# Transformer block with adaptive layer norm: exponentials' sums grouped up to the diagonal on GpSimd, splits of q and k moved to ScalarE and VectorE

## What is computed

```python
mod = silu(condition) @ Wada + bada                      # shift, scale, gate, twice
sh_a, sc_a, gt_a, sh_m, sc_m, gt_m = jnp.split(mod, 6, axis=1)
xm = layernorm(x) * (1.0 + sc_a[:, None, :]) + sh_a[:, None, :]
q, k, v = split heads of (xm @ Wqkv)                     # 16 heads of 32
scores = where(causal, q @ k.T * hd ** -0.5, -inf)
x = x + gt_a * ((softmax(scores) @ v) @ Wproj + bproj)
xm = layernorm(x) * (1.0 + sc_m[:, None, :]) + sh_m[:, None, :]
x = x + gt_m * (gelu(xm @ W1 + b1) @ W2 + b2)
```

## Time and profile before

| | |
|---|---|
| three executions | 3172.76, 3175.78 (median), 3176.37 us |
| span of the profiled execution | 3170.2 us |
| TensorE matmul busy | 3123.6 us, 99% |
| VectorE, GpSimd, ScalarE busy | 74%, 55%, 38% |
| one attention body with a block (13 of them) | 92.1 us |
| of that, GpSimd busy in 700 to 792 us | 76.6 us |

### The profile page before, as it was taken

One profiled execution on the slowest core, in us unless ns is written; L12 is line 12 of the kernel. 1 busy time (PEld: TensorE's weight loads), 2 busy tenths in 40 slices (PEclk: granted clock), 3 DMA queues, 4 the chain that ended last, 5 costly groups with the idle time before them and its releaser, 6 DMA issues.

```text
span 3170.2 us, 68318 instructions
## 1 busy us (share of the span) xinstructions
PE 3123.6 (99%) x24936; PEld 2518.4 (79%) x24936; DVE 2343.5 (74%) x2981; ACT 1196.1 (38%) x2354; POOL 1747.6 (55%) x1385
## 2 busy tenths in 40 slices
PE   7999999999999999999999999999999999999999
PEld 5677777777777777766688888989888898988888
DVE  4688887887888787766876777777677777767673
ACT  3355555555555555566521221212112121211111
POOL 3288888888888888888843333333332333323232
PEclk9999999999999999999999999999999999999999
DMA  6766666666656665666612312122221313122120
GB/s 241 217 185 192 173 191 185 180 181 186 195 171 191 186 182 168 195 194 171 167 57 64 75 44 79 40 79 56 63 75 44 79 40 79 56 63 74 45 66 14
DMA packets 304627, 391.85 MB, mean 124 GB/s; under 512 B 24296, under 2 KB 206088, under 8 KB 304448
## 3 DMA queue, kind: packets, MB, share of 16 engines
q1 hardware_dynamic: 292336, 371.86, 41.3%
q10 hardware_dynamic: 12112, 17.42, 1.6%
HBM read 270.66 MB, written 118.00 MB: 123 GB/s over the span
## 4 chain that ended last, share of the span: by engine, by line
PE 89%; DVE 5%; issue 2%; POOL 1%; ACT 1%; DMA 1%; SPq 0%; ACTq 0%; DVEq 0%; POOLq 0%
PE psH L1014 22%; PE psY L1024 22%; PE psA L793 9%; PE psT L847 8%; PE psA L885 7%; PE psP L922 6%; PE psA L797 6%; PE psS L816 4%; DVE mx L1364 2%; PE psA L858 2%; PE psA L765 1%; DVE psS L1360 1%; PE psA L907 1%; PE psA L902 1%; PE psA L847 1%
## 5 line engine op out<-in xcount | busy, mean ns | idle before, releaser
L1637 POOL TENSOR_TENSOR h_l<-h_full,h_h 128x256 fp32r<-128x256 f32 x512 | 488.9, 955 | 1073.5 <-DVE h_h L1537 1073.5
L1364 DVE TENSOR_REDUCE mx<-psS 128x4 f32<-128x2048 f32 (+3 forms) x384 | 665.9, 1755 | 119.5 <-PE psS L816 81.7
L1116 ACT ACTIVATE e<-psT 128x512 f32<-128x512 f32 (+1 forms) x1202 | 605.6, 554 | 375.0 <-PE psT L847 371.8
L1239 ACT ACTIVATE h_full<-psH,b1c 128x256 f32<-128x256 f32 x512 | 243.0, 475 | 1216.8 <-PE psH L1014 1216.8
L1014 PE MATMUL psH<-a_l,w1p_h 128*128 128x256 f32 x2048 | 576.1, 281 | 0.0
L1014 PE MATMUL psH<-a_h,w1p_l 128*128 128x256 f32 x2048 | 575.9, 281 | 0.0
L1014 PE MATMUL psH<-a_h,w1p_h 128*128 128x256 f32 x2048 | 574.1, 280 | 1.0 <-ACT o_sb L1124 0.8
L1695 POOL TENSOR_TENSOR es<-e 128x512 f32<-128x512 f32 (+1 forms) x242 | 446.7, 1847 | 159.3 <-ACT e L1116 75.4
L1537 DVE CAST h_h<-h_full 128x256 fp32r<-128x256 f32 x512 | 179.6, 351 | 399.5 <-ACT h_full L1239 396.8
L847 PEld LDWEIGHTS psT<-qst,kst 97*128 97x128 f32 x2404 | 349.0, 189 | 113.6 <-issue 70.7
L847 PE MATMUL psT<-qst,kst 97*128 97x256 f32 (+1 forms) x2404 | 410.4, 290 | 3.2 <-ACT e L1116 1.7
(11 more groups left out here) (120 smaller groups left out, 5211.2 us busy)
## 6 DMA issues: line engine op xcount, KB each, us to landing
qk_split<-qk_hl SPq DMA_DIRECT2D x128, 512.0 KB, 3.6
kst<-qk_split SPq DMA_DIRECT2D x128, 256.0 KB, 3.9
qst<-qk_split SPq DMA_DIRECT2D x128, 256.0 KB, 4.1
xin<-in_x_dram SPq DMA_DIRECT2D x64, 256.0 KB, 3.5
values<-vout ACTq DMA_DIRECT2D x64, 256.0 KB, 2.4
kmx<-qk_split SPq DMA_DIRECT2D x32, 512.0 KB, 4.7
qmx<-qk_split SPq DMA_DIRECT2D x32, 512.0 KB, 5.9
kst<-qk_split SPq DMA_DIRECT2D x128, 128.0 KB, 3.9
```

Source lines behind the costliest of these rows:

```text
L1116: act.activation(e[:, s % ERING, 2 * hp:2 * hp + 2, 0:w], score_bank(s, hp, with_a)[:, :, 0:w], ACT.Exp, scale=SCALE).then_inc(sem("exp_do ...
L1239: act.activation(h_full[:, m % 4, :], psH[:, m % 4, 0:RA], ACT.Gelu, bias=b1c[:, m:m + 1])\
L1364: reduce = dve.tensor_reduce(mx[:, part, :, qt], psS[:, :, col:col + w], AX_X, ALU.max)
L1637: return pool.tensor_tensor(dst, full, high.bitcast(F32), ALU.subtract)
```

## The change

Three things change, all within the bodies with a block.

1. The groups become (0,1,2,3), (4,5,6), (7,8), (9). The diagonal slots 3, 6 and 8 are now later slots of a group: each gets a `half_add` of 1024 elements before its 512-element addition. So GpSimd does 12 additions of 1024 elements in a half in place of 9. No group ends off the diagonal any more, so `added_sums` falls away in these bodies (3 in a half), and `diagonal_sums` for slots 3, 6 and 8 runs 4 x 256 columns on `es` in place of 2 x 4 x 128 on `e` and `es`.
2. The high part of q and k is taken by ScalarE (`a_high`: a copy, as it already is in the beginning) in the step in which VectorE took it.
3. The low part is subtracted by VectorE (`a_low`), in the step in which GpSimd did, and a store of q and k waits for VectorE's semaphore.

```diff
-SUM_GROUPS = {True: [(0, 1, 2), (3,), (4, 5)] + [(i,) for i in range(6, SLOTS)], False: [(i,) for i in range(SLOTS)]}
+SUM_GROUPS = {True: [(0, 1, 2, 3), (4, 5, 6), (7, 8), (9,)], False: [(i,) for i in range(SLOTS)]}
...
-                sp.wait_ge(sem("a_lo_done"), ia * A_NLO + n + 1)
+                if isinstance(ia, int) and ia < AHEAD:
+                    sp.wait_ge(sem("a_lo_done"), ia * A_NLO + n + 1)
+                else:
+                    sp.wait_ge(sem("a_lo_body"), (ia - AHEAD) * A_NLO + n + 1)
...
+            def a_high(ia, n):
+
+                act.wait_ge(sem("a_copied"), ia * A_ITEMS + n + 1)
+                act.activation(qk_hl[:, n % QK_RING, HIGH[n % 2]].bitcast(F32R), qk_hl[:, n % QK_RING, LOW[n % 2]],
+                               ACT.Copy).then_inc(sem("qk_hi"), 1)
...
+                    item = formed(u, s, 1, HIGH_LATE, with_a, after_a)
+                    if item and item[1] < A_NQK:
+                        a_high(*item)
                     if r in PLACE_AT and not (last and h + PLACE_AT[r][0] == 2):
...
-            def a_high(ia, n):
+            def a_low(ia, n):
 
                 if n < A_NQK:
-                    dve.wait_ge(sem("a_copied"), ia * A_ITEMS + n + 1)
-                    full = qk_hl[:, n % QK_RING, LOW[n % 2]]
-                    dve.tensor_tensor(qk_hl[:, n % QK_RING, HIGH[n % 2]].bitcast(F32R), full, full, ALU.max)\
-                       .then_inc(sem("qk_hi"), 1)
+                    dve.wait_ge(sem("qk_hi"), ia * A_NQK + n + 1)
+                    at = qk_hl[:, n % QK_RING, LOW[n % 2]]
+                    dve.tensor_tensor(at.bitcast(F32R), at, qk_hl[:, n % QK_RING, HIGH[n % 2]],
+                                      ALU.subtract).then_inc(sem("a_lo_body"), 1)
...
-                    item = formed(u, s, 1, HIGH_LATE, with_a, after_a)
+                    item = formed(u, s, 1, LOW_LATE, with_a, after_a)
                     if item:
-                        a_high(*item)
+                        a_low(*item)
...
-                    item = formed(u, s, 1, LOW_LATE, with_a, after_a)
-                    if item:
-                        a_low(*item)
```

More of the change, by code:

```diff
@@ L1194, in wqkv_high @@
                 act.activation(wqkv_h[:, :, cols], wqkv[:, :, cols], ACT.Copy).then_inc(sem("wqkv_hi"), 1)
[L1196 to L1200, removed]
             wqkv_high(0)
@@ L1211, in _ @@
                     if n < A_NQK:
-                        a_high_alone(ia, n)
+                        a_high(ia, n)
                     if n > A_NQK:
```

## The result

The changed kernel takes 3181.37 us (median of 11 runs, 3181.11 to 3184.88), the kernel before 3174.04 in the same rounds. The ratio is 1.0025 with a 95% interval of 1.0016 to 1.0034: 7 us slower. The sign is what I forecast, at a third of the size; the largest part of the loss came from another mechanism.

A forecast was written before the change was run, and what follows sets the result against it. TensorE was taken as the bound, its matmuls filling 99% of the span. Per body -2.76 + 1.35 + 0.35 + 1.85 + 0 + 0.8 + 0.3 = +1.9 us, over 12 bodies +22.8: 3198.5 us, range 3164 to 3220.

The forecast's parts named there:

- The sum: All gains and stalls of a body with a layer norm: +1.9 us, in 12 bodies +22.8 us.
- What TensorE is spared: Six `added_sums` of 0.46 us fall away in each body: 2.76 us off; joined diagonal matmuls gain 0.
- GpSimd's chain, steps 9 and 15: At slots 3 and 6, TensorE waits for GpSimd's masks and additions: stalls of 1.35 and 0.35 us.
- D: How much later TensorE stands than before: +0.9 us after step 9, +0.8 after step 15; also the forecast itself, chance 0.50.
- Step 19: At slot 8, behind `a_rstd`, TensorE stalls 2.15 us for GpSimd's chain, against 0.31 before: 1.85 more.
- the 746.7 for the chain without collisions: In step 19, GpSimd's chain without collisions ends at 746.7 and TensorE waits 1.06 us, 0.75 more than before.
- Step 39: At slot 8, the chain alone gives 0.1 us, two splits of the block about 0.9; taken as 0.8 (0.1 to 1.6).
- Meetings of VectorE and GpSimd: VectorE's instructions with two SBUF inputs do not overlap GpSimd's; each costs a backlogged GpSimd 0.47 us, layer-norm ones 0.2.
- rival B: VectorE becomes a bound as well, TensorE waiting for its maxima: +2.9 us a body, 3211 us; chance 0.15.
- Step 23: ScalarE's copy stands ahead of `a_modulate`, for which TensorE already waits: 0.3 us added (0 to 0.6).
- Rival A: Saved matmuls win because VectorE's instructions mostly find gaps in GpSimd's list: -1.2 us a body, 3160 us; chance 0.22.

The follow-up runs named there:

- the last two experiments: Changed kernel with the modulation ahead of the copy on ScalarE and only slot 6, or slots 3 and 6, joined: 0.9981 and 0.9974 of the kernel before.

## Why the prediction was right or wrong

The sum failed in two of its terms. GpSimd's chain, forecast at 4.35 us of stalls a body (steps 9, 15, 19 and 39), cost 1.31; and the wait of TensorE for VectorE's maxima, put at nothing, cost 1.75. One by one:

- **What TensorE is spared**: right. 6 x 0.46 was 6 x 0.44, and the joined diagonal matmuls cost nothing either way.
- **GpSimd's chain, steps 9 and 15** (1.35 and 0.35 us): wrong, 0 and 0 in the changed kernel. The chain was about as late as I had it: the addition of slot 3 ends 18.0 us behind the body's first addition, where I had 18.6. But TensorE wants it only at 18.7, because VectorE has made it 1.3 us late by then. The chain does cost where that is taken away: 0.44 in step 9 and 0.53 in step 15 with the first subtraction moved, 0.74 and 0.53 with the block's low part as zeros. TensorE stood 0.9 us later than before at the end of step 15, where I had D at 0.8: that is luck, since VectorE had made it late and not GpSimd.
- **Step 19** (2.15 us of stall): mis-sized, about 0.9. From the end of `a_rstd` at 745.13 to L910 at 750.79 it is 5.66 us, where my terms made 6.45. The wait of GpSimd for itself is 0.16 us between mask and addition, not 0.26; the two meetings cost 0.16 and 0.20 in masks that took 0.78 and 0.82, not 0.47, 0.2 and 0.2. Also `a_rstd` itself takes 1.02 us, not 1.39. One reading of mine does not add up: the 746.7 for the chain without collisions needs `a_rstd` to end 1 us earlier as well, which I did not say; from 742.3 its own terms give 747.7.
- **Step 39** (0.8): measured 0.72, from -0.44 to +0.28. It goes to nothing when the low part of the block is zeros, so the splits' share of it was right too.
- **Meetings of VectorE and GpSimd**: I had the right mechanism and gave it the wrong payer. I priced what a meeting costs GpSimd (0.47; measured 0.35 for the addition of 2.74 us) and let it go to L907. What it costs VectorE, up to 2.15 us, I put at 0, with 1 us as rival B. It measured 0.32 + 0.28 + 0.68 + 0.47 = 1.75 us a body. The reason that I gave, 1 to 2 us of idle time ahead of many maxima, does not carry that far: ahead of the maxima of step 5 VectorE had idled for 1.08 us in the kernel before, half of the 2.15 that the meeting costs, and in steps 3 and 11 TensorE already waited for the maxima then (with step 23 these are the three waits of the earlier trace rows). The Trainium skill (SBUF — State Buffer, Who interferes with whom) says that a VectorE instruction with two SBUF inputs contends with a GpSimd instruction that reads SBUF, that the shared port pair is an exclusive lock, and that the order of issue decides who blocks. The 2.83 and 2.75 us agree with that rule, and the 0.69 and 0.71 of the same instructions when they start first do too.
- **Step 23** (0.3, at most 0.6): measured 0.41, half of it from ScalarE's order and half (0.20) from TensorE's wait for the row maxima in that step.
- **The sum**: -2.76 and +4.65 were forecast, -2.64 and +3.5 measured (0.59 and 0.72 at steps 19 and 39, 1.75 for VectorE, 0.41 for step 23). The stalls did not add: TensorE waits once for whoever is last. I carried D through GpSimd's chain, but not through VectorE's.

Rival A's condition, stalls below 2.76 us a body, was missed by 0.7. Rival B's mechanism was at work, in D's place instead of on top of it. That the loss was smaller than the sum of both is the covering that the moved subtraction shows.

For L1347 the two kinds of body in the kernel with short half additions show that the order of arrival is the cause and not the length of the instruction. For L1354 and steps 7 and 11 it rests on the kernels in which the same instruction came first; none of them changes that order alone without moving anything else. What I did not try is a kernel with a different grouping in each half of a body, which the last two experiments point to.

## What to carry to other kernels

Where two engines exclude each other, cost a moved instruction for both: what it makes the one wait and what it makes the other wait, and look behind each for the wait that is already tight. Moving the list of the one engine can lengthen a single instruction of the other by nearly a whole instruction of the first, and which one is hit depends on tenths of a microsecond, so step-by-step differences between two timelines say more than any total. And stalls of several engines at one in-order engine hide each other: after removing one, look for what it covered.

## What the runs showed of the hardware

- A VectorE subtraction of 128 x 512 with both inputs in SBUF takes 0.68 us alone. It took 2.83 us when a GpSimd addition of 2.39 us had started 0.11 us earlier, and 0.71 us when it started 0.24 us ahead of one, which then took 2.71. Writing zeros over the same columns took 0.49 us throughout.
- Giving GpSimd 13 us less to do in a body of 93 did not make the kernel faster. Within that kernel, a body took 93.3 us or more where VectorE's two-input instruction started 0.3 us behind GpSimd's addition, and 89.4 or 89.7 where it started 1.1 us ahead. With VectorE's four such instructions for the block taken out of each body, the mean was 89.3.
- In the kernel with short half additions the granted clock fell to the lower level behind two waits of TensorE, of 1.14 and 2.10 us, in six bodies of the nine that had them (0.57 from 622 to 626 us); such a body took 1.1 to 2.4 us longer than the other three.
- GpSimd waits 0.16 us for its own semaphore between one mask and the addition behind it (0.26 behind two masks in a row).
